# A decoder layer on one core: key softmax in the same program part as the projections, output chunks between the memory update's halves, last tile's scaling on VectorE

## The reference, cut to what matters

```
step(carry, qkv):                       # sub-layer 1, scanned over segments of 128 tokens
    sq = elu(qs) + 1
    mem = mem + einsum('bhsk,bhsv->bhkv', sq, vs)
    zc = zc + (elu(ks) + 1).sum(-2)
    att_dot = softmax(qs ks^T * scale) @ vs
    att = gate * (sq @ mem) / (sq.sum * zc) + (1 - gate) * att_dot
    out_seg = att @ Wo
x = layernorm(x + attn(x))
x = layernorm(x + cross_attention(x, context 4 x 77 x 192))   # sub-layer 2, 16 heads of 64
# sub-layer 3, 16 heads of 16
q, k, v = split_heads(x @ Wq), split_heads(x @ Wk), split_heads(x @ Wv)
scores = einsum('bqd,bkd->bkq', q, k) / sqrt(D)
attn = softmax(scores, axis=-1)         # over the queries, for each key
z = einsum('bkq,bkv->bqv', attn, v) @ Wo
z = gelu(l2norm(l2norm(z) @ Wff))
out = layernorm(x + z)
```

## Time and profile before

| | us |
|---|---|
| three timed runs | 1865.12, 1869.35, 1875.42 (median 1869.35) |
| the profiled execution | 1863.79 |
| its span in the trace | 1862.0 |
| segment attention, iterations | from about 20 to 790, 48 each |
| cross attention and thirds | to 1201 |
| key softmax | 1206 to 1796 |
| output block | to 1862 |

### The profile page before, as it was taken

The page is one execution under the profiler, slowest core; times in us unless marked ns, Lnnn a source line. Parts: engine busy times, 40 slices in busy tenths (PEclk is TensorE's granted clock), DMA queues, the critical chain, the costliest instruction groups (busy, mean ns, idle before and its releaser), DMA issues. The chain is left out here.

```text
span 1862.0 us, 43234 instructions
## 1 busy us (share of the span) xinstructions
PE 1782.5 (96%) x16262; PEld 1203.0 (65%) x16262; DVE 1441.0 (77%) x2683; ACT 1527.4 (82%) x4485; POOL 705.0 (38%) x812
## 2 busy tenths in 40 slices
PE   6999999999999999899999999899999999999995
PEld 5888888888888888768999998722222222222244
DVE  6677777777777777546666666599999999999967
ACT  6777777777777777737888885599999999999987
POOL 2344333343344444403766650032332332333325
PEclk9999999999999999999999999999999999999998
DMA  7233322332322332442011005833355335434202
GB/s 176 52 62 65 61 65 57 63 64 57 62 62 62 63 56 54 87 127 81 25 37 45 16 13 117 245 46 47 47 71 67 46 51 77 57 46 63 29 1 91
DMA packets 140591, 121.65 MB, mean 65 GB/s; under 512 B 78923, under 2 KB 112607, under 8 KB 140383
## 3 DMA queue, kind: packets, MB, share of 16 engines
q1 hardware_dynamic: 140383, 118.88, 32.8%
HBM read 77.29 MB, written 41.53 MB: 64 GB/s over the span
## 5 line engine op out<-in xcount | busy, mean ns | idle before, releaser
L2066 DVE TENSOR_REDUCE s_neg_max<-s_ring 128x1 f32<-128x1024 f32 x512 | 580.0, 1209 | 7.5 <-PE s_ring L1959 7.3
L2001 ACT ACTIVATE s_prob<-s_ring,s_neg_max 128x1024 f32<-128x1024 f32 x512 | 569.8, 1114 | 7.8 <-DVE s_neg_max L2066 6.5
L1972 PE MATMUL s_acc<-s_prob,s_v_norm 128*32 128x256 f32 x4096 | 325.7, 391 | 1.9 <-POOL s_v_norm L2043 1.9
L1959 PE MATMUL s_ring<-f_stack 128*128 128x512 bf16 x1024 | 313.2, 388 | 11.4 <-PEq L2366 5.3
L2039 POOL TENSOR_TENSOR s_row_inv<-s_row_sum,s_neg_one 128x4 f32<-128x4 f32 x128 | 128.8, 1006 | 381.8 <-ACT s_prob L2001 381.8
L608 POOL TENSOR_SCALAR a_relu_ring<-a_qT 128x512 f32<-128x512 f32 x64 | 98.6, 1557 | 343.2 <-ACT a_qT L475 315.9
L1972 PEld LDWEIGHTS s_acc<-s_prob,s_v_norm 128*32 128x32 f32 x4096 | 81.3, 108 | 217.9 <-issue 214.3
L1959 PEld LDWEIGHTS s_ring<-f_stack 128*128 128x128 bf16 x1024 | 58.9, 97 | 236.5 <-ACT s_prob L2001 222.5
L504 ACT ACTIVATE a_prob<-a_psum,a_neg_max 128x128 f32<-128x128 f32 x512 | 179.4, 398 | 21.4 <-DVE a_neg_max L724 21.4
L767 DVE SCALAR_TENSOR_TENSOR a_att<-a_psum,a_keep_cols,a_num_s 128x128 f32<-128x128 f32 x256 | 72.1, 344 | 131.5 <-ACT a_num_s L530 131.5
L1324 ACT ACTIVATE x_prob<-x_psum,x_neg_max 128x77 f32<-128x77 f32 x512 | 160.8, 339 | 15.9 <-DVE x_neg_max L1482 15.9
(11 more groups left out here) (207 smaller groups left out, 4112.2 us busy)
## 6 DMA issues: line engine op xcount, KB each, us to landing
f_stack<-qk_thirds SPq DMA_DIRECT2D x256, 128.0 KB, 6.8
segment_values<-a_v_stage SPq DMA_DIRECT2D x64, 256.0 KB, 3.2
a_v_pos<-segment_values SPq DMA_DIRECT2D x512, 32.0 KB
qk_thirds<-p_third SPq DMA_DIRECT2D x16, 768.0 KB, 8.2
a_x_in<-in_x_dram SPq DMA_DIRECT2D x16, 256.0 KB, 3.2
a_x_res<-in_x_dram SPq DMA_DIRECT2D x32, 128.0 KB, 2.8
after_attention<-a_normed SPq DMA_DIRECT2D x32, 128.0 KB, 2.4
x_x_in<-after_attention SPq DMA_DIRECT2D x32, 128.0 KB, 2.1
```

Of the source, the lines that this page charges most:

```text
L1959: last = pe.matmul(ring[n % 3][:, f * HALF:(f + 1) * HALF], k_stack[:, slot, j, kt * P:(kt + 1) * P], q_stack[:, slot, j, f * HALF:(f + 1) ...
L1972: last = pe.matmul(acc[32 * j:32 * j + 32, s], v_norm[:, step // KT % 2, step % 4, j, :], prob[:, step % 4, j, s], start=step % (2 * KT) = ...
L2001: act.activation(prob[:, step % 4, j, :], ring[n % 3][:, :], ACT.Exp, bias=neg_max[:, step % 2, j:j + 1], accum_out=row_sum[:, step % 4, j ...
L2066: dve.tensor_reduce(neg_max[:, step % 2, j:j + 1], ring[n % 3][:, :], AX_X, ALU.max, negate=True).then_inc(max_ready, 1)
```

## The change

1. *Preparation, PE.* Before, the output chunks 12 to 15 all stood ahead of the four memory products. Now chunks 12 and 13 stand ahead of units 0 and 1, and chunks 14 and 15 between these and units 2 and 3. *VectorE* now adds the memory of units 0 and 1 ahead of `phi_inverse(it, 2)`, and those of units 2 and 3 ahead of `phi_inverse(it, 3)`; the residual stands between.
2. *The key softmax moves into the first block.* `emit_key_softmax` becomes `key_softmax`, whose five parts are called behind `query_thirds`. Its PSUM tiles are those of the thirds, its SBUF tiles get places beside theirs. The first three score tiles wait for what the thirds still do with these PSUM banks; GpSimd's clearing of `v_norm` waits for the value products of batch 2. One barrier goes; the one with the clearing of semaphores now stands between softmax and output block.
3. *Last tile.* For the last of the 128 steps VectorE takes the reciprocal and the product that GpSimd did.
4. Some semaphores are merged (`gate_step`, `high_made`), with no instruction more or less.

```diff
@@ run_pe, preparation
                 if it > 0:
-                    project_out(pe, it - 1, range(12, H))
-                for u in range(UNITS):
-                    memory(it, u)
+                    project_out(pe, it - 1, range(12, 14))
+                memory(it, 0)
+                memory(it, 1)
+                if it > 0:
+                    project_out(pe, it - 1, range(14, H))
+                memory(it, 2)
+                memory(it, 3)
                 turn_phin(it, 0)
@@ run_dve, preparation
                 inverse(it, 1)
-                phi_inverse(it, 2)
                 add_memory(it, 0)
                 add_memory(it, 1)
                 if it > 0:
                     residual(it - 1)
-                phi_inverse(it, 3)
+                phi_inverse(it, 2)
                 add_memory(it, 2)
                 add_memory(it, 3)
+                phi_inverse(it, 3)
                 inverse(it, 2)
@@ emit_attentions
+    softmax = key_softmax(nc, parts, memory, shared, stack_landed, B, S)
...
             thirds[1](pe)
+            softmax[1](pe)
@@ key_softmax, run_pe
                 if n >= 3:
                     pe.wait_ge(exp_done, n - 2)
+            elif n == 2:
+                pe.wait_ge(values_taken, 2 * B - 1)
+            else:
+                pe.wait_ge(rests, 4 * B - 1 + n)
...
+            if piece == 0 and step < B * STEPS - 1:
+                pe.wait_ge(vnorm_ready, step + 1)
+            elif piece == 0:
+                pe.wait_ge(last_ready, 2)
+            if step == 0 and piece == 0:
+                pe.wait_ge(values_taken, 2 * B)
@@ key_softmax, run_pool
+        pool.wait_ge(values_done, 2 * (B - 1))
+        pool.memset(v_norm[:, :, :, :, :].rearrange("p a b c d -> p (a b c d)"), 0.0).then_inc(c_set, 1)
...
+                if n == B * STEPS - 1:
+                    break
@@ key_softmax, run_dve
+        n, step, group = B * STEPS - 1, STEPS - 1, GROUPS - 1
+        at = group % 2 * HD
+        dve.wait_ge(exp_done, 4 * n + 4)
+        dve.reciprocal(last_inv[:, :], row_sum[:, step % 4, :]).then_inc(last_ready, 1)
+        dve.wait_ge(last_ready, 1)
+        dve.tensor_tensor(v_norm[:, group % 2, step % 4, :, at:at + HD],
+                          v_all[:, B - 1, KT - 1, group * 4 * HD:(group + 1) * 4 * HD].rearrange("p (h d) -> p h d", d=HD),
+                          last_inv[:, :].unsqueeze(2).to_broadcast([P, 4, HD]), ALU.mult).then_inc(last_ready, 1)
         take_right(B * ZC - 1)
```

More of the change, by code:

```diff
@@ L1597, in _ @@
             thirds[0](sp)
+            softmax[0](sp)
         @block.tensor
@@ L1611, in _ @@
             thirds[2](act)
+            softmax[2](act)
         @block.gpsimd
@@ L1616, in _ @@
             cross[3](pool)
+            softmax[3](pool)
         @block.vector
@@ L1622, in _ @@
             thirds[3](dve)
+            softmax[4](dve)
 HD = D // H
@@ new lines, in key_softmax, with run_sp, run_pe, scores @@
+    high_made, last_ready = sem("high_made"), sem("last_ready")
+    def run_sp(sp):
+        for b in range(B):
+            for group in range(GROUPS):
+                if b > 0 or group >= 2:
+                    sp.wait_ge(scores_done, b * TURNS + (group - 1) * (TURNS // GROUPS))
+                    load_stacks(sp, parts, b, group, group % 2, stacks, stack_landed)
+    def run_pe(pe):
+        def scores(b, step, j):
+            n = b * TURNS + step * 4 + j
+            slot, kt = (step // KT) % 2, step % KT
+            if n >= 3:
+                pe.wait_ge(exp_done, n - 2)
+            elif n == 2:
+                pe.wait_ge(values_taken, 2 * B - 1)
+            else:
+                pe.wait_ge(rests, 4 * B - 1 + n)
+            for f in range(2):
+                last = pe.matmul(ring[n % 3][:, f * HALF:(f + 1) * HALF],
+                                 k_stack[:, slot, j, kt * P:(kt + 1) * P],
+                                 q_stack[:, slot, j, f * HALF:(f + 1) * HALF], start=True, stop=True)
+            last.then_inc(scores_done, 1)
+        def values(step, piece):
+            s = slice(piece * PIECE, (piece + 1) * PIECE)
+            chunk = step // (2 * KT)
+            if piece == 0 and step < B * STEPS - 1:
[4 more added lines that the diff above has]
+                pe.wait_ge(values_taken, 2 * B)
+            if piece % 2 == 0 and step % (2 * KT) == 0 and chunk > 0:
+                pe.wait_ge(zT_ready[piece // 2], chunk)
+            for j in range(4):
+                last = pe.matmul(acc[32 * j:32 * j + 32, s], v_norm[:, step // KT % 2, step % 4, j, :],
+                                 prob[:, step % 4, j, s], start=step % (2 * KT) == 0 and piece % 2 == 0,
+                                 stop=step % (2 * KT) == 2 * KT - 1, skip_group_check=True)
+            if piece % 2 == 1:
+                last.then_inc(half_done[piece // 2], 1)
+        for b in range(B):
+            for step in range(STEPS):
+                if step % KT == 0:
+                    pe.wait_ge(stack_landed[(step // KT) % 2], b * (2 * NSTACK) + (step // KT // 2 + 1) * NSTACK)
+                for j in range(4):
+                    scores(b, step, j)
+                    if b * STEPS + step >= 2:
+                        values(b * STEPS + step - 2, j)
+        for step in range(B * STEPS - 2, B * STEPS):
+            for j in range(4):
+                values(step, j)
@@ new lines, in run_act, with take_left @@
+    def run_act(act):
+        def take_left(chunk):
+            act.wait_ge(half_done[0], (chunk + 1) * 2 * KT)
+            act.copy(zT_all[:, chunk // ZC, chunk % ZC, 0:HALF], acc[:, 0:HALF]).then_inc(zT_ready[0], 1)
+        for b in range(B):
+            for step in range(STEPS):
+                for j in range(4):
+                    n = b * TURNS + step * 4 + j
+                    act.wait_ge(max_ready, n + 1)
+                    act.activation(prob[:, step % 4, j, :], ring[n % 3], ACT.Exp,
+                                   bias=neg_max[:, step % 2, j:j + 1],
+                                   accum_out=row_sum[:, step % 4, j:j + 1]).then_inc(exp_done, 1)
+                    if n // 4 % (2 * KT) == 1 and j == 0 and n // 4 > 1:
+                        take_left(n // (8 * KT) - 1)
+        take_left(B * ZC - 1)
@@ new lines, in run_dve, with take_right @@
+    def run_dve(dve):
+        def take_right(chunk):
+            dve.wait_ge(half_done[1], (chunk + 1) * 2 * KT)
+            dve.tensor_copy(zT_all[:, chunk // ZC, chunk % ZC, HALF:S], acc[:, HALF:S]).then_inc(zT_ready[1], 1)
+        for b in range(B):
+            for step in range(STEPS):
+                for j in range(4):
+                    n = b * TURNS + step * 4 + j
+                    dve.wait_ge(scores_done, n + 1)
+                    dve.tensor_reduce(neg_max[:, step % 2, j:j + 1], ring[n % 3], AX_X, ALU.max,
+                                      negate=True).then_inc(max_ready, 1)
+                if n // 4 % (2 * KT) == 1 and n // 4 > 1:
+                    take_right(n // (8 * KT) - 1)
+        n, step, group = B * STEPS - 1, STEPS - 1, GROUPS - 1
+        at = group % 2 * HD
+        dve.wait_ge(exp_done, 4 * n + 4)
[4 more added lines that the diff above has]
+                          last_inv[:, :].unsqueeze(2).to_broadcast([P, 4, HD]), ALU.mult).then_inc(last_ready, 1)
+        take_right(B * ZC - 1)
```

244 lines of the change are left out of this document (86 added, 158 removed).

## The result

| | before | changed |
|---|---|---|
| first comparison, 12 runs each | 1869.43 (1865.12 to 1876.43) | 1857.70 (1854.07 to 1865.16) |
| ratio | | 0.9939 (95% interval 0.9927 to 0.9952) |
| second comparison, 12 and 7 runs | 1869.82 | 1860.42, ratio 0.9954 (0.9938 to 0.9971) |
| profiled execution | 1863.79, span 1862.0 | 1858.56, span 1856.8 |

The change makes the kernel 11.4 us faster by the first comparison (13.6 to 9.0) and 8.6 by the second (11.6 to 5.4). 1855.9 was forecast for 1857.7, within the range 1850 to 1866. The sum came near, but its terms for the attention reorder and for the second boundary were wrong in ways that the traces show.

What follows compares the result with a forecast made beforehand. TensorE's work and few waits were taken to bound segment attention, with VectorE and ScalarE filling the softmax. Terms −8.2 − 5.8 − 0.9 + 1.4 = −13.5 took the median 1869.35 to 1855.9 us, range 1850 to 1866.

Steps and rivals of the forecast that it cites:

- attention reorder: Segment attention: moved chunks remove TensorE's wait for VectorE's add, 0.54 us in each of 13 iterations; −8.2 in all, bounds 0 and 9.
- second boundary: Between softmax and output block: clearing semaphores there adds 1.4 us, bounds 1.3 and 1.8.
- The added changes cost nothing beyond 0.09 per iteration: Segment attention: two added changes between kinds of matmul cost 0.09 us, already counted in the 4.08 us stretch.
- the estimate by the rule: Segment attention: unhidden weight loads cost some 0.2 us more per iteration; reorder brings about 5.4, time 1858.7; left out of the sum.
- The first iteration gains 0.78: First iteration of segment attention: no chunks, but the add moves ahead of a sum costing 0.78 us, gaining that.
- The last iteration gains 0.3: Last iteration of segment attention: TensorE then waits for GpSimd's product; gain between 0 and 0.54 us, taken as 0.3.
- my slower rival: Segment attention: VectorE's residual delays the sums of units 2 and 3, 1.0 us per iteration; total +9.7, 1879; chance 0.05.
- The third iteration's 0.13: Third iteration of segment attention: its wait is already shorter, so only 0.13 us is left to win.
- First boundary: Between last projection and softmax: without the barrier the first score comes 5.3 us earlier; −5.8 in all, bounds 4.2 and 6.1.
- the sign that I had named: Start of softmax: PEclk stays 1.00 in its first ten microseconds if the forecast is right.
- Last tile: End of softmax: reciprocal and product on VectorE take 0.5 us with hand-over, not 1.43; −0.9, bounds 0.6 and 1.0.
- the rival of the clock: Second boundary: TensorE's idle grows to about 2.5 us and its clock falls, costing up to 5; 1860.9; chance 0.08.

Runs made afterwards that it cites:

- e5: Changed kernel with output chunks at two more places between transposes per iteration, four more changes between 64 and 128 rows, no matmul added; ratio 0.9992 to the kernel before.
- f3: e8 run again: changed kernel with segment attention's semaphores cleared by GpSimd inside the softmax, not at the second boundary; ratio 0.9919 to the kernel before.
- e4: Changed kernel with the last tile's reciprocal and product on GpSimd again, as before; ratio 0.9948 to the kernel before.
- f1: The kernel before, unchanged, run again for a second trace; its profiled execution took 1867.51 us.
- e2: Changed kernel with the preparation's order as before, softmax in the first block and last tile on VectorE kept; ratio 0.9975 to the kernel before.
- e6: Changed kernel with four unused score matmuls added on TensorE behind the last value product; ratio 0.9941 to the kernel before.
- e8: Changed kernel with segment attention's semaphores cleared by GpSimd inside the softmax and no clearing at the second boundary; ratio 0.9937 to the kernel before, 5 runs.
- e9: Changed kernel with the semaphores cleared inside the softmax and VectorE's sum of unit 3 ahead of the adds; ratio 0.9915 to the kernel before.
- e3: Changed kernel with VectorE's sum of unit 3 ahead of the adds of units 2 and 3 again; ratio 0.9943 to the kernel before.
- f4: e9 run again: semaphores cleared inside the softmax and the sum of unit 3 early; ratio 0.9921 to the kernel before.

## Why the prediction came out

**Attention reorder, −8.2 forecast.** The traces give, on the mean of three with the old order and ten with the new (all but e5): second iteration −0.43, third −0.03, the next twelve −5.1 (576.63 to 571.49). The first iteration, from its L334 to chunk 12 of the second, took 47.59 and 47.55 with the old order and 48.80, 47.19, 48.33, 46.80 and 46.89 with the new one where no dip was in it: 0.0 on the mean. The last one, from chunk 12 on, took 33.34 either way. Sum −5.6; timed −7.1 (−9.9 to −4.3). Three steps failed.
- *The added changes cost nothing beyond 0.09 per iteration.* I had measured a group of chunks that follows scores, which also use 64 rows. The added group follows memory products of 128 rows, and this kind of change was not in the row I used. The stretch is 4.20 and not 4.08, 0.42 of gain and not 0.54. Over 13 iterations that is 1.6 of the missing 2.6. I had also said that the row disagrees with the rule of the Trainium skill ("TensorE: Matmul & The Clock Gate", Part 3, The mechanism), by which a weight load overlaps running matmuls only when their rows differ. My row spoke of most loads in the mean; it could not speak of a load at a change. By the rule I had estimated 0.2 more per iteration and 5.4 us for the reorder. The runs show 0.12 and 5.6, and e5 0.13 per change, near the 107 ns that the formula of the same page of the Trainium skill, in its section on LDWEIGHTS, gives for 128 columns. So the estimate by the rule was nearer than mine. That unhidden loads are the reason is not shown: the change back to L334, whose weights have 64 columns and not 128, costs 0.10 as well (0.306 instead of 0.209). And within one kind the trace disagrees with the rule: the scores of L1967 above all use 128 rows and have a load each, and five of them run in 1.24 us.
- *The first iteration gains 0.78.* It gains nothing on the mean, because there TensorE mostly waits for the transfer of `a_v_pos` and not for the add (last section). Where that wait was short the forecast gain is there: 46.80 in f3, 0.8 less than before.
- *The last iteration gains 0.3.* It gains 0. VectorE's new order makes the sum of unit 3 later (GpSimd's product begins 387.50, I had worked out an end of 387.9 and it ended 388.55), and this is the mechanism of my slower rival. In the other iterations the projections cover it; in the last there are none, and L345 of unit 3 comes 7.52 behind chunk 12 as before. The rival had its place right and its extent wrong: once and not fifteen times, and no more than the gain.

The third iteration's 0.13 did not come either, since what its wait had left was eaten by the change of rows.

**First boundary, −5.8 forecast:** −5.8 in every trace without the barrier, though its parts were 5.2 and 0.6 and not 5.3, 0.4 and 0.1. The value copy did not hold the third tile. But the sign that I had named, PEclk 1.00 in the softmax's first ten microseconds, stands in both traces of the changed kernel and in no other of the eleven without the barrier, and in seven of these the softmax gives 1.0 to 2.2 us back (last section). **Last tile, −0.9:** −0.98, by e4.

**Second boundary, +1.4 forecast:** +1.92 for the clearing. SyncE's wait there is 1.8. More semaphores are cleared than before, but GpSimd's clearing itself takes 0.88 us and took 0.83; where the other 0.5 comes from is open.

```profile
SPq L2390 <- PEq L2390: 1.8, 1, 1.8
```

The upper bound was 1.8, so the 1.92 is just outside it. Here too came, with the likeliest case and not in its place, the rival of the clock: the output block takes 66.66 to 67.13 in the seven traces that have the clearing there, and 65.29 to 65.48 in the seven that don't. I gave it 0.08 with a price of up to 5. It should have been likely: idle time went from 1.08, behind which the clock stayed at 1.00, toward the 5.25 behind which it was at 0.50, and no row stood between.

**The sum.** −5.6 − 5.8 − 0.98 + 1.92 + 1.7 = −8.8 by undisturbed stretches, against −13.5. Timed, it is −11.4 (−13.6 to −9.0) and −8.6 (−11.6 to −5.4). So the forecast's closeness to 1857.7 is in part luck: its errors of 2.6 and 2.2 are partly cancelled by a first comparison that is kinder than the traces. Whether dips come more seldom in the changed kernel, which would close the gap between −8.8 and −11.4, is open; the second comparison doesn't need it.

## What to carry to other kernels

Price a move of matmuls by the neighbours it gets, not by the matmuls: here each place where 64-row and 128-row weights meet costs 0.10 to 0.13 us of TensorE, and four more of them per iteration cost 7 us by the traces, most of what the change had brought. When an engine's order is rotated, look at the first and the last iteration separately, since there the cover is missing, and measure from a mark that the edit doesn't move: from the first L334 the last iteration seemed to lose 0.86 us, from chunk 12 it loses nothing. When a barrier or a clearing moves, price the idle time it makes for TensorE's clock as well; and put the clearing where GpSimd is idle anyway.

## What the runs showed that was not expected

The first iteration is bound by a transfer. In ten of the eleven traces with the new order TensorE's wait ahead of the third unit's memory product is one for `a_v_pos`, of 1.2 to 4.8 us, and in f1, the kernel before, it is too (3.3). The first trace of before had 1.9 for the add there, e2 1.8. Waits of the second changed trace and of f3, the eleventh, in their first iteration:

```profile
PE a_psum L334 <- DMA a_v_pos<-segment_values: 4.8, 1, 4.8
```

```profile
PE a_psum L335 <- DVE a_mem L759: 1.1, 1, 1.1
```

So the first iteration's gain is what the transfer leaves. This is seen, not tested: no run moved the transfer. The clock dips of that iteration come with these waits: seven of the eight traces that wait 3.1 us or more have one, and none of the six that wait up to 2.6.

The softmax takes 584.72 us in the two traces whose clock stays at 1.00 at its start, both of the changed kernel. Its cost follows how long the half level lasts beyond the first value products, which start 8.7 to 9.3 us behind the first maximum. Without the barrier the clock falls 3.3 to 5.2 us behind the first maximum in the other nine traces. Where it is back by 8.1 us (e2, e4) the softmax takes 584.92; where it is back at 10.8 to 12.0 (e5, e6, e8, e9; the first window of e6 above lies in such a dip) 585.7 to 586.2; where it is back at 13.5 (e3, f3, f4) 586.9. With the barrier the clock is at 0.50 before the softmax begins and back by 5.9 to 9.7, and the softmax takes 584.92 to 585.22. Why the clock falls behind a start without a barrier in some executions and not in others is open.
